# Gathering raw token rows with their moments, a norm split over VectorE and GpSimd, and a rounded output product

## The chip, the cores and the metric

The kernel runs on one core of one Trainium2 chip. The metric is the device time of the whole program in microseconds (us), taken as the median of several executions. The core has TensorE (matmuls into PSUM), VectorE, ScalarE, GpSimd and SyncE, which run their own instruction streams and meet through semaphores, and 16 DMA engines, fed here by SyncE's queue (q1) and by GpSimd's (q0). In profile rows TensorE is PE (its weight loads PEld), VectorE is DVE, ScalarE is ACT, GpSimd is POOL, SyncE is SP.

## The reference

The input x is 32 batches of 512 tokens with 256 features. With xn the layernorm of x over the features, the result is x + attention(xn) + experts(xn):

```python
xn = _layernorm(x, axis=-1)                       # (x - m) / sqrt(v + 1e-5)
# attention: 16 heads of 16, relative positions
q, k, val = heads(xn @ Wq + bq), heads(xn @ Wk + bk), heads(xn @ Wv + bv)
pos = _sinusoid_pos_emb(S, D) @ Wp + bp
score = ((q + u) @ k.T + relative_shift((q + v) @ pos.T)) / 4
att = (softmax(score) @ val) @ Wo + bo
# experts: 8, each takes its 128 best tokens of a batch
probs = softmax(xn @ gate_w); g, m = top_k(probs.T, 128)
h = gelu(xn[m] @ w1) @ w2                         # 256 -> 1024 -> 256
ffn = zeros.at[m].add(g * h)
return x + att + ffn.astype(bfloat16)
```

## The kernel before

The program has two blocks, `attention_phase` and `ffn_phase`.

**The norm stage** opens `attention_phase`: 32 steps, one batch each, over four buffers. A batch of x lies in SBUF as 128 partitions of four tokens. Per batch SyncE loads x (L335), VectorE takes statistics (L679, L682), ScalarE the root of the variance (L541), VectorE the reciprocal (L687) and then the norm, four tensor_scalars of 256 columns (L693). TensorE turns the result (8 transposes, L872), ScalarE copies it from PSUM (L548), TensorE computes expert scores (L881). SyncE stores the normed rows to `xn_d` (L339) and the turned ones to `xt_d` (L343). The normed rows in DRAM are for the expert gathers; the turned ones are read again by the attention loop. Between these steps stand, at fixed batch numbers, position projections (b 2 to 10), and the first value, query and key products (b 14 to 31). At b 6 to 9 ScalarE's copy of a spread position (L585) stands ahead of its next root in its program.

**The attention loop**, 16 iterations of two batches, goes through heads; its scores travel through DRAM for the relative shift. At its end GpSimd issues the first eight expert gathers, with VectorE, TensorE and ScalarE still at the last heads.

**The expert stage**, `ffn_phase`: 8 experts times 8 groups of four batches, so 64 groups t of 512 tokens. For a group, GpSimd gathers four times 128 rows of `xn_d` with an indirect DMA (L92), TensorE turns them (`turn`, L1535), ScalarE and VectorE split them into a rounded high part and the rest (L1390, L1432); then eight times f: the up product in three rounded partial products (L1553), gelu twice on ScalarE (L1407, L1409), a subtraction on VectorE for the low part of h (L1472), and half of a down product of the group before (L1514), whose output tile VectorE scales by the probability (L1440, every second f) and GpSimd scatters with accumulation to `ffn_d` (L1347). VectorE asks nothing of the gathers; TensorE waits for them ahead of `turn`, at f=1 of the group before.

Everything in this stage is in program order, written by hand. GpSimd's loop over t is: gather(t+2), prepare, scatter(t-1), where gather(t+2) waits for `turn` of group t and each scatter for its output tile.

Experts 1 to 4 are the mixed part: each group also carries one batch of attention output. SyncE loads heads, inverse sums and x (`load_mid`), GpSimd multiplies heads by inverse sums and adds the bias to x (`prepare`, L1353, L1354), TensorE multiplies by Wo at f=5 (`times_wo`, L1524), into the PSUM tile that `turn` uses, VectorE adds x (L1457, f=6) and SyncE stores. The product is in plain f32:

```python
ins = pe.matmul(ap[:, t], att[:, g % 2, c, t * P:(t + 1) * P], wo[:, c], start=(c == 0), stop=(c == DC - 1))
```

## Time and profile before

| | us |
|---|---|
| median of 3 runs | 4815.69 (4812.66 to 4815.7) |
| the profiled execution | 4826.3 |
| its span, first to last instruction | 4824.4 |
| TensorE busy in it | 4458.8 |
| VectorE busy | 3669.3 |
| ScalarE busy | 3441.5 |
| GpSimd busy | 1710.0 |

The norm stage runs from 0 to 147 us of the span, the attention loop's start to about 200 and the loop to 3169, the expert stage from 3175, its mixed part from about 3240 to 4100. A busy time is the union of an engine's instructions; an engine that waits inside an instruction counts as busy. Columns named "idle before" give the time in which an engine stood idle ahead of a group of instructions and what ended most of it. GB/s counts every byte that a DMA moves once.

### The profile page before, as it was taken

What the parts mean: (1) busy time and instruction counts of PE and PEld (TensorE: products, weight loads), DVE (VectorE), ACT (ScalarE), POOL (GpSimd) and SP (SyncE); (2) the same over time, 40 slices, a digit from 0 to 9 for tenths busy, and PEclk for the clock granted to TensorE, in tenths of its full rate; (3) what the DMA queues carried; (4) which work ended last, traced back from release to release, by engine and by line L of the source; (5) the groups of instructions that cost most, each with busy time, mean ns of one, the idle gap of its engine ahead of it and who ended that gap; (6) DMA issues with size and microseconds to landing.
All of it is one profiled execution on the core that took longest, in us unless ns stands there. A gap on an engine that the chain in (4) does not pass through costs nothing. (4 is left out here: it accounts for less than half of the span.)

```text
span 4824.4 us, 127659 instructions
## 1 busy us (share of the span) xinstructions
PE 4458.8 (92%) x50604; PEld 3425.4 (71%) x50604; DVE 3669.3 (76%) x8040; ACT 3441.5 (71%) x5180; POOL 1710.0 (35%) x1545
## 2 busy tenths in 40 slices
PE   7799998989999999999999989879999999999997
PEld 3466666666666666666666666669999999999997
DVE  7699999999999999999999998954554545534344
ACT  3699999999899999999898999844333434344454
POOL 0222322222232232222323222234565656544443
PEclk9899999999999999999999999989999999999999
DMA  9899999999999999999999999973555545433259
GB/s 341 334 368 377 379 374 376 376 372 378 373 383 378 378 382 375 377 377 377 372 373 379 373 372 374 365 249 65 119 135 118 146 108 145 96 63 84 48 158 316
DMA packets 394088, 1390.59 MB, mean 288 GB/s; under 512 B 51104, under 2 KB 128800, under 8 KB 327712
## 3 DMA queue, kind: packets, MB, share of 16 engines
q1 hardware_dynamic: 270624, 778.39, 44.5%
q0 software_dynamic: 122880, 604.05, 38.3%
q8 instruction: 412, 6.75, 0.6%
q14 instruction: 172, 1.41, 0.1%
HBM read 708.00 MB, written 674.23 MB: 287 GB/s over the span
## 5 line engine op out<-in xcount | busy, mean ns | idle before, releaser
L604 ACT ACTIVATE att_shifted<-att_shifted,att_mn 128x512 f32<-128x512 f32 x2048 | 1362.2, 719 | 0.2 <-DVE att_mn L740 0.2
L740 DVE CUSTOM_DVE_ANT_0 att_shifted<-att_quad,att_shifted 128x512 f32<-128x512 f32 x2048 | 1324.2, 683 | 50.1 <-PE att_quad L984 41.7
L599 ACT ACTIVATE ring<-att_quad 128x1024 f32<-128x1024 f32 x1024 | 1049.3, 1025 | 207.0 <-PE att_quad L972 204.7
L750 DVE COPY att_pt<-att_tp 128x512 f32<-128x512 f32 x1536 | 1009.8, 685 | 157.1 <-PE att_tp L1010 142.9
L490 POOL DMA_DIRECT2D att_shifted<-xs_d x512 | 279.3, 546 | 2102.5 <-DMA xs_d<-ring 1817.1
L1472 DVE TENSOR_TENSOR ffn_hp<-ring,ffn_hp 128x512 fp32r<-128x512 f32 x512 | 477.5, 933 | 686.6 <-ACT ring L1409 646.5
L1009 PEld LDWEIGHTS att_tp<-ident,att_shifted 64*128 64x128 f32 x8192 | 597.3, 140 | 517.1 <-ACT att_shifted L604 393.3
L1407 ACT ACTIVATE ffn_hp<-ffn_up 128x512 fp32r<-128x512 f32 x512 | 305.9, 597 | 915.6 <-PE ffn_up L1553 905.8
L1009 PE MATMUL att_tp<-ident,att_shifted 64*128 64x64 f32 x8192 | 727.7, 229 | 204.4 <-DVE att_pt L750 197.9
L972 PE MATMUL att_quad<-att_pos,att_qv 64*128 64x512 f32 x2048 | 870.0, 445 | 15.8 <-ACT ring L599 15.6
L984 PE MATMUL att_quad<-att_kd,att_qu 64*128 64x512 f32 x2048 | 826.7, 451 | 50.8 <-DVE att_mn L740 39.6
L1514 PE MATMUL ffn_yp<-ffn_w2p,ffn_hp 128*128 128x256 f32 x6144 | 827.8, 284 | 3.4 <-DVE ffn_hp L1472 1.7
L1514 PEld LDWEIGHTS ffn_yp<-ffn_w2p,ffn_hp 128*128 128x128 f32 x6144 | 798.7, 191 | 41.0 <-DVE ffn_hp L1472 3.8
L1553 PE MATMUL ffn_up<-ffn_xp,ffn_w1p 128*128 128x512 f32 x3072 | 795.5, 394 | 2.8 <-DVE ffn_xp L1432 2.8
L1010 PE MATMUL att_tp<-ident,att_shifted 64*128 64x64 f32 x8192 | 738.9, 231 | 2.9 <-issue 2.9
L1347 POOL DMA_INDIRECT ffn_d<-ring,picks x256 | 431.5, 1686 | 696.5 <-DVE ring L1440 683.0
L1553 PEld LDWEIGHTS ffn_up<-ffn_xp,ffn_w1p 128*128 128x128 f32 x3072 | 546.5, 190 | 93.6 <-DVE ffn_xp L1432 3.2
L1010 PEld LDWEIGHTS att_tp<-ident,att_shifted 64*128 64x128 f32 x8192 | 597.0, 140 | 4.3 <-issue 3.0
L984 PEld LDWEIGHTS att_quad<-att_kd,att_qu 64*128 64x128 f32 x2048 | 363.9, 187 | 303.2 <-DVE att_mn L740 182.2
L1027 PE MATMUL att_op<-att_pt,att_val 128*17 128x128 f32 x16384 | 564.8, 278 | 11.1 <-issue 7.1
L1027 PEld LDWEIGHTS att_op<-att_pt,att_val 128*17 128x17 f32 x16384 | 411.2, 98 | 170.6 <-issue 161.2
L972 PEld LDWEIGHTS att_quad<-att_pos,att_qv 64*128 64x128 f32 x2048 | 365.9, 186 | 68.1 <-ACT ring L599 21.6
(113 smaller groups left out, 5312.2 us busy)
## 6 DMA issues: line engine op xcount, KB each, us to landing
xs_d<-ring SPq DMA_DIRECT2D x1024, 513.0 KB, 8.9
att_shifted<-xs_d POOLq DMA_DIRECT2D x512, 1024.0 KB, 9.6
att_shifted<-in_L_attn_x_dram SPq DMA_DIRECT2D x32, 512.0 KB, 7.2
xn_d<-att_shifted SPq DMA_DIRECT2D x32, 512.0 KB, 6.3
xt_d<-att_shifted SPq DMA_DIRECT2D x32, 512.0 KB, 7.4
gathered<-xt_d SPq DMA_DIRECT2D x32, 512.0 KB, 12.1
att_d<-att_osb SPq DMA_DIRECT2D x512, 32.0 KB
ring<-in_L_ffn_w_dram SPq DMA_DIRECT2D x16, 1024.0 KB
```

Of the source, the lines that this page charges most:

```text
L599: act.activation(xo[:, kk % NW, 2 * half:2 * half + 2, 1:S + 1], xp[:, :, :], ACT.Copy).then_inc(x_out, 1)
L604: act.activation(shifted[:, kk % NX, t], shifted[:, kk % NX, t], ACT.Exp, bias=mn[:, kk % NX, t:t + 1], scale=-1.0).then_inc(exp_done, 1)
L740: dve.tensor_tensor_reduce(out=shifted[:, kk % NX, t], in0=sp_[:, t % 2], in1=shifted[:, kk % NX, t], scale=-0.25, scalar=-NEG, op0=ALU.ad ...
L750: dve.tensor_copy(turned_to(t // 2, t % 2), tp[:, t % 2]).then_inc(t_out_dve, 1)
L972: ins = pe.matmul(xp[:, t % 2, :], qv[rows, kk // GH % 2, t * P:(t + 1) * P], pos[rows, kk // GH % NG8, :], start=True, stop=True)
L984: pe.matmul(sp_[:, t % 2, :], qu[rows, kk // GH % 2, t * P:(t + 1) * P], kd[rows, kk // GH % 2, :], start=True, stop=True).then_inc(s_full, 1)
L1009: low = pe.transpose(tp[:, 0, at], shifted[0:ROWS, kk % NX, t, keys], ident[0:ROWS, 0:ROWS])
L1010: high = pe.transpose(tp[:, 1, at], shifted[ROWS:P, kk % NX, t, keys], ident[ROWS:P, ROWS:P])
L1027: ins = pe.matmul(op[32 * t:32 * t + HD + 1, kk % QH * P:(kk % QH + 1) * P], val[:, kk // H % 2, c, kk % H, :], pt[:, c, t * P:(t + 1) * P ...
L1472: dve.tensor_tensor(hp[:, g % 2, 1, f], hf[:, f % 2], hp[:, g % 2, 0, f].bitcast(F32), ALU.subtract).then_inc(h_low, 1)
L1514: ins = pe.matmul(yp[:, k % 2, 0:D], hp[:, g % 2, hi, f, k * CAP:(k + 1) * CAP], w2p[:, wi, f, :], start=(f == 0 and s == 0), stop=(f == F ...
L1553: ins = pe.matmul(up[:, f % 4, :], w1p[:, wi, c, f * P:(f + 1) * P], xp[:, g % 2, xi, c, :], start=(s == 0 and c == 0), stop=(s == 2 and c ...
```

## The change

- **Norm stage.** The normed rows are no longer stored. The mean and the inverse deviation of every token stay in a tile `st` and are stored to `st_d`, 8 bytes a token, for eight batches at a time. Of a batch's four norm instructions VectorE makes two and GpSimd two (`normed_too`). GpSimd's later work of this stage (the split of the first batch, of queries and keys) now stands between its norms, behind b=11, 24 and 27.
- **Gathers.** Each gather becomes two, of the token's moments from `st_d` and of its raw row from x.
- **Norm of gathered rows.** VectorE norms them in place, four tensor_scalars per group, for group t+2 at f=5, 6, 7 of group t; `turn` waits for them. The first two groups are normed at the end of `attention_phase`.
- **Output product.** Wo and the divided heads are split into rounded high parts (ScalarE) and low parts (VectorE), and the product is made of three partial products, 24 matmuls per batch in place of 8. The heads are split at f=0 of the group, Wo once in expert 0. `prepare` moves one group earlier.

```diff
-def gather_tokens(pool, xn_d, picks, xg, e, g, k):
-    return pool.indirect_dma_start(xg[:, g % 2, k], None, xn_d, bass.IndirectOffsetOnAxis(ap=picks[:, g * GB + k, e:e + 1], axis=0))
+def gather_tokens(pool, of_token, picks, tile, e, g, k):
+    return pool.indirect_dma_start(tile[:, g % 2, k], None, of_token, bass.IndirectOffsetOnAxis(ap=picks[:, g * GB + k, e:e + 1], axis=0))
+
+
+def normalise_tokens(dve, xg, moments, g, k):
+    of_row = moments[:, g % 2, k]
+    return dve.tensor_scalar(xg[:, g % 2, k], xg[:, g % 2, k], of_row[:, 0:1], of_row[:, 1:2], ALU.subtract, ALU.mult)
...
                 for b in range(B):
-                    store_xn(b)
                     if b + NS < B:
+                        sp.wait_ge(normed, b + 1)
+                        sp.wait_ge(normed_too, b + 1)
                         load_x(b + NS)
+                    if b % MOMENTS == MOMENTS - 1:
+                        store_moments(b + 1 - MOMENTS, b + 1)
                     if b:
                         store_xt(b - 1)
...
+                def normalise(b):
+                    k = b % NS
+                    wait_alone(pool, recip, b + 1)
+                    wait_alone(pool, turned, b - NS + 1)
+                    for t in range(TT // 2, TT):
+                        ins = pool.tensor_scalar(xn[:, k, t], xin[:, k, t], st[:, b, t, 0:1], st[:, b, t, 1:2], ALU.subtract, ALU.mult)
+                    ins.then_inc(normed_too, 1)
...
-                    dve.reciprocal(rstd[:, k], sd[:, k]).then_inc(recip, 1)
+                    dve.reciprocal(st[:, b, :, 1], sd[:, k]).then_inc(recip, 1)
                     dve.wait_ge(recip, b + 1)
 
-                    wait(dve, xn_stored[k], b // NS * 16)
                     wait(dve, turned, b - NS + 1)
-                    for t in range(TT):
-                        ins = dve.tensor_scalar(xn[:, k, t], xin[:, k, t], mv[:, k, t, 0:1], rstd[:, k, t:t + 1], ALU.subtract, ALU.mult)
+                    for t in range(TT // 2):
+                        ins = dve.tensor_scalar(xn[:, k, t], xin[:, k, t], st[:, b, t, 0:1], st[:, b, t, 1:2], ALU.subtract, ALU.mult)
                     ins.then_inc(normed, 1)
...
+                for g in range(2):
+                    dve.wait_ge(shared.x_in[g], GB * 32)
+                    for k in range(GB):
+                        normalise_tokens(dve, xg, moments, g, k).then_inc(shared.x_ready, 1)
...
                     for k in range(GB):
-                        gather_tokens(pool, xn_d, picks, xg, e, g, k).then_inc(x_in[g % 2], 16)
+                        gather_tokens(pool, st_d, picks, moments, e, g, k).then_inc(x_in[g % 2], 16)
+                        gather_tokens(pool, x.rearrange("b s d -> (b s) d"), picks, xg, e, g, k).then_inc(x_in[g % 2], 16)
...
-                    if MIX * NG <= t < MIX * NG + B:
-                        prepare(t - MIX * NG)
+                    if MIX * NG - 1 <= t < MIX * NG - 1 + B:
+                        prepare(t - (MIX * NG - 1))
...
+                def split_att(b, s):
+                    act.wait_ge(divided, b + 1)
+                    wait(act, a_full, b)
+                    act.activation(attp[:, 0], att[:, s], ACT.Copy).then_inc(a_high, 1)
...
+                def normalise(t, k):
+                    g = t % NG
+                    if k == 0:
+                        dve.wait_ge(x_in[g % 2], (t // 2 + 1) * (GB * 32))
+                    normalise_tokens(dve, xg, moments, g, k).then_inc(x_ready, 1)
...
+                def split_att(b, s):
+                    dve.wait_ge(a_high, b + 1)
+                    dve.tensor_tensor(attp[:, 1], att[:, s], attp[:, 0].bitcast(F32), ALU.subtract).then_inc(a_low, 1)
...
+                            if f >= 5 and t + 2 < NE * NG:
+                                for k in {5: (0,), 6: (1,), 7: (2, 3)}[f]:
+                                    normalise(t + 2, k)
...
-                    pe.wait_ge(divided, b + 1)
+                    pe.wait_ge(a_low, b + 1)
                     pe.wait_ge(x_low, e * NG + g + 2)
                     for t in range(TT):
-                        for c in range(DC):
-                            ins = pe.matmul(ap[:, t], att[:, g % 2, c, t * P:(t + 1) * P], wo[:, c], start=(c == 0), stop=(c == DC - 1))
+                        for n, (ai, wi) in enumerate(SPLITS):
+                            for c in range(DC):
+                                ins = pe.matmul(ap[:, t], attp[:, ai, c, t * P:(t + 1) * P], wop[:, wi, c],
+                                                start=(n == 0 and c == 0), stop=(n == 2 and c == DC - 1))
```

How the program order moves at the places that matter. First GpSimd in the norm stage, before (`att_shifted` holds x and xn, `att_xt` the split first batch, `att_qc` and `att_kc` the split queries and keys):

```order
L480 CAST att_xt<-gathered 128x1024
L482 TENSOR_TENSOR att_xt<-gathered,att_xt 128x1024
L450 CAST att_qc<-att_qn 128x512
L452 TENSOR_TENSOR att_qc<-att_qn,att_qc 128x512
L470 CAST att_kc<-att_qn 128x512
L472 TENSOR_TENSOR att_kc<-att_qn,att_kc 128x512
L450 CAST att_qc<-att_qn 128x512
L452 TENSOR_TENSOR att_qc<-att_qn,att_qc 128x512
```

and now:

```order
L514 TENSOR_SCALAR att_shifted<-att_shifted,att_st 128x256 x24
L497 CAST att_xt<-gathered 128x1024
L499 TENSOR_TENSOR att_xt<-gathered,att_xt 128x1024
L514 TENSOR_SCALAR att_shifted<-att_shifted,att_st 128x256 x26
L467 CAST att_qc<-att_qn 128x512
L469 TENSOR_TENSOR att_qc<-att_qn,att_qc 128x512
L514 TENSOR_SCALAR att_shifted<-att_shifted,att_st 128x256 x6
L487 CAST att_kc<-att_qn 128x512
L489 TENSOR_TENSOR att_kc<-att_qn,att_kc 128x512
L467 CAST att_qc<-att_qn 128x512
L469 TENSOR_TENSOR att_qc<-att_qn,att_qc 128x512
L514 TENSOR_SCALAR att_shifted<-att_shifted,att_st 128x256 x8
```

GpSimd's 64 norm instructions stand around its splits, which only followed each other before.

Second, VectorE from f=5 of a mixed group to f=1 of the next, where w2 isn't split, before (`ffn_hp` is the split h, `ring` the output tile, `ffn_tokens` x plus attention):

```order
L1472 TENSOR_TENSOR ffn_hp<-ring,ffn_hp 128x512 x2
L1440 TENSOR_SCALAR ring<-ffn_yp,chosen 128x256
L1472 TENSOR_TENSOR ffn_hp<-ring,ffn_hp 128x512
L1457 TENSOR_TENSOR ffn_tokens<-ffn_tx,ffn_tokens 128x1024
L1472 TENSOR_TENSOR ffn_hp<-ring,ffn_hp 128x512
L1440 TENSOR_SCALAR ring<-ffn_yp,chosen 128x256
```

and now (`gathered` holds the gathered rows, `ffn_attp` the split heads):

```order
L1500 TENSOR_SCALAR ring<-ffn_yp,chosen 128x256
L103 TENSOR_SCALAR gathered<-gathered,moments 128x256
L1540 TENSOR_TENSOR ffn_hp<-ring,ffn_hp 128x512
L1525 TENSOR_TENSOR ffn_tokens<-ffn_tx,ffn_tokens 128x1024
L103 TENSOR_SCALAR gathered<-gathered,moments 128x256
L1540 TENSOR_TENSOR ffn_hp<-ring,ffn_hp 128x512
L1500 TENSOR_SCALAR ring<-ffn_yp,chosen 128x256
L103 TENSOR_SCALAR gathered<-gathered,moments 128x256 x2
L1540 TENSOR_TENSOR ffn_hp<-ring,ffn_hp 128x512
L1518 TENSOR_TENSOR ffn_attp<-ffn_heads,ffn_attp 128x1024
```

Four norms and the split of the heads come in; the norm of k=1 stands ahead of the last subtraction of h.

## Rows read from the trace of the kernel before

**Rows 1.** Stretch; busy of PE, PEld, DVE, ACT, POOL; granted clock, DMA share, GB/s.

```profile
60.00:70.00 10.00, 7.50 (x18) 3.07 (x17) 4.75 (x18) 3.08 (x6) 2.32 (x1) 0.67 0.58 167
```

**Rows 2.** The same of three longer stretches.

```profile
75.00:110.00 35.00, 32.23 (x144) 15.37 (x142) 30.47 (x125) 12.91 (x21) 0.00 (x0) 1.00 1.02 413
...
3240.00:4100.00 860.00, 860.00 (x5399) 778.50 (x5398) 425.89 (x492) 332.45 (x595) 492.76 (x318) 1.00 0.52 123
4100.00:4740.00 640.00, 640.00 (x4119) 581.81 (x4118) 279.39 (x396) 282.65 (x498) 308.33 (x221) 1.00 0.43 103
```

**Rows 3.** DMA issues of the first 280 us, KB each, us to landing.

```profile
xn_d<-att_shifted SPq DMA_DIRECT2D x32, 512.0 KB, 6.3
```

**Rows 4.** Timeline of the norm stage: start, us, engine, line, idle before.

```profile
75.57 1.38 DVE L693 TENSOR_SCALAR att_shifted<-att_shifted,att_osb 128x256 f32<-128x256 f32 x4
...
78.78 1.38 DVE L693 TENSOR_SCALAR att_shifted<-att_shifted,att_osb 128x256 f32<-128x256 f32 x4
...
109.34 1.26 ACT L563 ACTIVATE att_qn<-att_mp,att_bias_q 128x512 f32<-128x512 f32 x2
...
110.76 1.25 POOL L450 CAST att_qc<-att_qn 128x512 fp32r<-128x512 f32 x1 [48.44 <-ACT att_qn L563]
...
110.98 1.18 DVE L693 TENSOR_SCALAR att_shifted<-att_shifted,att_osb 128x256 f32<-128x256 f32 x1
...
115.44 1.10 PE L872 MATMUL att_quad<-ident,att_shifted 128*128 128x128 f32 x8 [0.29 <-DVE att_shifted L693]
...
118.29 1.66 PE L911 MATMUL att_mp<-att_xt,att_wqkv 128*128 128x512 f32 x6
...
143.71 1.38 DVE L693 TENSOR_SCALAR att_shifted<-att_shifted,att_osb 128x256 f32<-128x256 f32 x4
```

**Rows 5.** Waits of the first 147 us: total, times, longest.

```profile
PE att_quad L872 <- DVE att_shifted L693: 33.7, 19, 10.1
...
DVE att_osb L679 <- DMA att_shifted<-in_L_attn_x_dram: 14.3, 14, 3.3
DVE att_osb L687 <- ACT att_osb L541: 14.0, 5, 5.3
```

**Rows 6.** Chain of waits in one mixed group: start, us, what.

```profile
3609.62 0.87 PE ffn_tx L1535 x8
...
3621.78 3.45 PE ffn_tx L1524 x16
...
3633.69 1.43 PE ffn_yp L1514 x12
...
3636.52 0.87 PE ffn_tx L1535 x8
```

**Rows 7.** Groups by line in the expert stage.

```profile
L1347 POOL DMA_INDIRECT ffn_d<-ring,picks x115 | 195.7, 1702 | 288.5 <-DVE ring L1440 282.9 <-issue 5.5
L92 POOL DMA_INDIRECT gathered<-xn_d,picks x116 | 123.5, 1065 | 35.4 <-issue 35.4
...
L1432 DVE TENSOR_TENSOR ffn_xp<-ffn_tx,ffn_xp 128x1024 fp32r<-128x1024 f32 x59 | 71.8, 1217 | 6.9 <-issue 5.1 <-ACT ffn_xp L1390 1.8
```

**Rows 8.** Timeline of the same mixed group, VectorE and GpSimd.

```profile
3614.47 5.69 DVE L1472 TENSOR_TENSOR ffn_hp<-ring,ffn_hp 128x512 fp32r<-128x512 f32 x1 [2.02 <-ACT ring L1409]
3614.84 2.42 POOL L1353 TENSOR_TENSOR ffn_heads<-ffn_heads 128x1024 f32<-128x1024 f32 x1
3617.20 2.39 POOL L1354 TENSOR_TENSOR ffn_tokens<-ffn_tokens,ffn_bob 128x1024 f32<-128x1024 f32 x1
...
3632.02 0.69 DVE L1472 TENSOR_TENSOR ffn_hp<-ring,ffn_hp 128x512 fp32r<-128x512 f32 x1 [0.99 <-ACT ring L1409]
```

**Rows 9.** GpSimd's groups in the first 280 us.

```profile
L482 POOL TENSOR_TENSOR att_xt<-gathered,att_xt 128x1024 fp32r<-128x1024 f32 x3 | 7.1, 2365 | 0.2
...
L480 POOL CAST att_xt<-gathered 128x1024 fp32r<-128x1024 f32 x3 | 3.1, 1036 | 54.9 <-DMA gathered<-xt_d 54.9
...
L470 POOL CAST att_kc<-att_qn 128x512 fp32r<-128x512 f32 x3 | 2.0, 667 | 11.6 <-ACT att_qn L570 8.9 <-PE att_mp L896 2.7
```

More of the change, by code:

```diff
@@ L154, in attention_phase @@
         xg = shared.tokens()
+        moments = shared.of_tokens()
         spread_at = (QH // GH * HD, QH // GH * HD + MH // GH * P + HD)
@@ L234, in attention_phase @@
         kept = m.sem("kept")
-        xn_stored = [m.sem(f"xn_stored{s}") for s in range(NS)]
+        st_stored = m.sem("st_stored")
+        normed_too = m.sem("normed_too")
         xt_stored = [m.sem(f"xt_stored{s}") for s in range(NS)]
@@ L490, in read_x @@
                     pool.dma_start(shifted[:, slot], xs_d[slot][S:S + S * S].rearrange("(p t c) -> p t c", t=TT, c=S)).then_inc(x_shifted[slot], 16)
-                split_xt(0, 0)
-                pool.wait_ge(p_out_dve, NG8 // 2)
-                pool.wait_ge(p_out_act, NG8 // 2)
-                with_v(0, 0)
-                keys(0, 0)
-                with_u(0, 0)
+                def normalise(b):
[5 more added lines that the diff above has]
+                    ins.then_inc(normed_too, 1)
+                for b in range(B):
+                    normalise(b)
+                    if b == 11:
+                        split_xt(0, 0)
+                    if b == 24:
+                        pool.wait_ge(p_out_dve, NG8 // 2)
+                        pool.wait_ge(p_out_act, NG8 // 2)
+                        with_v(0, 0)
+                    if b == 27:
+                        keys(0, 0)
+                        with_u(0, 0)
                 pool.wait_ge(p_low, DC)
@@ L527, in _ @@
                 pool.wait_ge(xt_low, B)
-                for n in range(NS):
-                    pool.wait_ge(xn_stored[n], 16 * (B // NS))
+                pool.wait_ge(st_stored, 16 * (B // MOMENTS))
                 by_batch = picks[:, :].rearrange("p (b e) -> p b e", e=NE)
@@ L1181, in ffn_phase @@
         att, inv = heads[:, 0:2], heads[:, 2:4]
+        sums = heads[:, 2:4].rearrange("p n c t -> p (n c t)")
         xi, mid = tokens[:, 0:2], tokens[:, 2:4]
```

66 lines of the change are left out of this document (46 added, 20 removed).

## The prediction

> **What bounds the kernel now.** I read the stages first [rows 1, 2], then in each stage the groups, the waits and the chain.
>
> The norm stage, the first 147 us, has no engine at its limit for long, but the DMA engines are: 75 to 110 us shows a DMA share of 1.02 at 413 GB/s, with TensorE at 32.2 of 35 us and VectorE at 30.5 [rows 2]. Each batch moves 512 KB three times, x in, xn out, xt out [rows 3]: 3 x 0.524 MB / 413 GB/s = 3.8 us. Eighteen batches, from VectorE's norm at 75.57 to the one at 143.71, took 68.1 us, 3.79 each [rows 4]. VectorE alone does a batch in 3.20 us (75.57 to 78.78) and waited 14.3 us in all for x [rows 4, 5]. Between 40 and 70 us another limit rules: batches 7 to 10 come slowly, because ScalarE's root of the next batch stands behind its copy of a spread position, VectorE's reciprocal waits for the root (14.0 us), and TensorE for the norm (33.7 us) [rows 5]. TensorE's granted clock is 0.67 of full as the mean of 60 to 70 us, between its levels of 1.2 and 2.4 GHz [rows 1].
>
> The attention loop (200 to 3130 us) is not touched.
>
> The expert stage belongs to TensorE: busy 860.00 of 860 us at clock 1.00 in the mixed part and 640.00 of 640 after it [rows 2]; the chain of waits there is TensorE's own matmuls, back to back [rows 6]. Whatever TensorE sheds comes off the end; whatever else is added there costs nothing unless it makes TensorE wait.
>
> **The output product, 32 times.** Before: eight f32 matmuls of 128x256, 3.45 us [rows 6]. Now 24 rounded ones with the same shape as the down product (a 128x128 weight load, 256 columns), of which twelve take 1.43 us on the chain [rows 6]: 24 x 1.43/12 = 2.86 us. Saved 0.59 us x 32 = **18.9 us**. It is on the path all of it. Bound above: the weight loads could be what paces them, but the down product has one load per matmul too, so 2.86 includes that. Bound below: nothing suggests less than 1.43/12.
>
> The product now needs more beside it. ScalarE gets a copy of 128x1024 at f=0 and VectorE a subtraction of that size, 1.22 us as the one it makes for xp [rows 7]; both have idle time there (VectorE 426 busy of 860 us, ScalarE 332 [rows 2]). The prepare on GpSimd is moved one group ahead, so that this fits: nothing.
>
> **The gathers.** Each group's four gathers become eight, four of raw rows and four of 8-byte moment rows. GpSimd needs for one gather 1.065 us and 0.31 us before it (35.4/116) [rows 7]; with the same price for the moments (same number of indices) eight take 11.0 us. Then prepare 4.8 us [rows 8], four scatters of 1.70 [rows 7] with some 0.2 between (an estimate), 7.7 us. Sum 23.5 us per mixed group, under TensorE's 26.9 - 0.6 = 26.3 us (the turn at 3609.62 to that at 3636.52 [rows 6]). The last scatter waits for the group's last output tile, so gathers start some 3 to 4 us into a group and have landed by about 17 us of it. VectorE asks for them at f=5, about 18 us in. Cover 1 to 2 us in the groups without product, more in the mixed ones: nothing on the path, but thin. Bounds: nothing, or up to 1 us a group in the 64 if landing is late and half of it shows.
>
> **The norm of gathered rows.** Four VectorE tensor_scalars per group, 1.38 us as the four in the norm stage [rows 4]. The tight place is the order at f=6: subtraction 6, the output tile, one norm, then subtraction 7, which TensorE needs for the next down product. Today it starts at 3632.02 and is done at 3632.71, TensorE comes to it at 3633.69 [rows 6, 8]: 1.0 us of slack against 0.35 us added. Where a group also splits w2 (once per expert) it can run out: I put in 0.3 us x 8, **+2 us** with the rest of such places. The first such norm, in the first group of all, waits for gathers that share the DMA with the zeroing of the accumulator in DRAM: +0 to +2, in the same figure.
>
> One behaviour matters more. In a mixed group a VectorE subtraction of two SBUF tiles that takes 0.69 us lasted 5.69 us: GpSimd's two tensor_tensors ran from 3614.84 to 3619.59, and it ended 0.57 us after them [rows 8]. So VectorE stood still for whole GpSimd instructions. It is hidden now (TensorE did not pause), and moves from f=3 to about f=5, where the product's 2.86 us cover it.
>
> **The norm stage.** Removed: 32 stores of 512 KB, so DMA needs 2 x 0.524/413 = 2.54 us per batch; SP loses 32 issues and gains four small ones. The limit passes to an engine. TensorE needs 2.85 us per batch: the turn starts at 115.44, the scores follow, and the next product starts at 118.29 [rows 4]. VectorE gives two of four tensor_scalars (0.69 us) to GpSimd. If both could run at once it would need 2.5 us. But they read SBUF at once: with GpSimd's cast in front of it (110.76 to 112.01) one VectorE tensor_scalar lasted 1.18 us instead of 0.35 [rows 4]. Both shares start from the same reciprocal, VectorE right behind it, GpSimd some 0.16 us later (the time from ScalarE's end, 110.60, to GpSimd's cast, 110.76 [rows 4]), so VectorE's second one waits for both of GpSimd's: 0.16 + 2P + 0.1 + 0.34 = 2P + 0.6 us, in place of 1.38, and a batch is 3.20 - 1.38 + 0.6 + 2P = 2.42 + 2P.
>
> P, a GpSimd tensor_scalar of 256 columns, stands in no row. Nearest are its casts, 667 ns for 512 columns and 1036 for 1024 [rows 9]: 0.72 ns a column and 0.30 fixed, so 0.48 us. Lower bound: VectorE's own 0.35. Upper: as two-input ops go, 2.37 us for 1024 columns [rows 9], some 0.7 for 256. I take 0.48, as it has one tensor input like the cast. Then 3.38 us per batch, 18 x 3.38 = 60.8. GpSimd's splits for queries and keys (2.8 and 4.7 us, now between two norms) hold VectorE's share up for some 5.5 us more than now: 66.3 against 68.1, -1.8. Before batch 13: the fifth load of x is issued 0.4 us earlier and lands without stores beside it, -2; the four serial batches keep their 1.38 us of norm as 1.56, +0.7. With the last stores gone in front of the first positions -1. **Sum -4 us**; with P at 0.35 it is -9, with 0.7 it is +4.
>
> The GPSIMD Engine Reference of the Trainium skill (section "When to use GPSIMD") calls one-input elementwise work on GpSimd roughly line-rate with VectorE; by it P would be near 0.35 and the sum 5 us lower, while the cast rows speak for 0.48.
>
> **The hand-over to the experts.** Sixteen gathers in place of eight, 22 us instead of 11, lie beside attention's last heads, and VectorE's eight norms, 2.8 us, beside its last stores. Nothing, bounds -2 and +3.
>
> **Sum.** -18.9 + 2 - 4 = -21 us. The profiled execution took 4826.3 us (span 4824.4), so 4805; the median of the runs is 10.6 us under it, and I predict from that: 4815.7 - 21 = **4794.5 us**, -0.44%.
>
> **Rivals.**
> A. Norm stage at TensorE's pace (17%). For it: TensorE was busy 92% at 75 to 110 us. Against: the 1.18 us row. 18 x 2.85 + 5 for its extra products (6 of them, the one at 118.29 takes 1.5) = 56 against 68, with the start -13: total -30, 4786.
> B. GpSimd's share is slow and the norm stage longer (15%). For it: VectorE stands still for all of it. P = 0.7 to 1.0 gives 3.8 to 4.4 us per batch, +4 to +15 us: total -13 to -2, 4803 to 4814.
> C. GpSimd's queue becomes the bound of the mixed part, slower than before (5%). Place: gathers, prepare and scatters in one queue, 23.5 of 26.3 us. It decides from (26.3 - 12.5)/8 = 1.72 us per gather with its gap, against 1.37 in the rows. If gathers cost what scatters do (1.70 + 0.3), a group is 28.5 us, 1.6 more than now: +51 - 4, 4863. Against: it needs 45% more per gather. The page "DMA: Bandwidth & Descriptors" of the Trainium skill (quick facts) wants 512 bytes or more per transfer, below which it speaks of a read-modify-write. No row here shows what an 8-byte row costs; it would burden the landing, and so the thin cover above.
> D. The product doesn't shrink (3%): three times the weight loads eat what the rounding saves. It stays at 3.45 us, total +2 - 4, 4814; against it the down product's 1.43.
> The forecast itself has 60%.
>
> **How the numbers follow.** A measurement tells about 0.2% (9.6 us) from no change. The forecast's own range: -9 to +4 in the norm stage for -4, 0 to 6 for the 2, so 4788 to 4803. The range that leaves out no more than C, D and the ends of A and B: 4781 to 4811. Faster by over 0.2% (under 4806): all of the forecast, A, a third of B: 0.81. Within: the rest of B and D, 0.13. Slower: C and what I don't see, 0.06.
>
> **What would show it.** Right: 24 matmuls of the product in about 2.86 us; TensorE busy all of the mixed part, groups 26.3 us apart; norms of the first stage 3.4 us apart after batch 12, with no wait of the statistics for x and VectorE tensor_scalars stretched to 1 us or more; DMA share there near 0.75. Wrong: TensorE idle before its turn or down product (late gathers), GpSimd without idle time in the mixed part, norms 4 us apart or 2.9, or a product of 3.4 us.

## The result, and the profile after

| | before | changed |
|---|---|---|
| median, us | 4814.17 (4 runs, 4807.62 to 4815.7) | 5234.77 (4 runs, 5232.59 to 5239.27) |
| span of the profiled execution, us | 4824.4 | 5234.9 |
| mean granted clock of TensorE | 0.982 | 0.933 |

The ratio is **1.0879**, 95% interval 1.0867 to 1.0892: 8.8% slower, where 0.44% faster was forecast. The time lies outside the range of 4781 to 4811.

I cut each execution at two instructions of TensorE: its first score product and its first transposition in the experts. These two rows are from the timeline of the changed kernel (start us, us, engine, line; idle before):

```profile
190.33 0.79 PE L1017 MATMUL att_quad<-att_kd,att_qu 64*128 64x512 f32 x1
...
3589.78 1.94 PE L1612 MATMUL ffn_tx<-ident,gathered 128*128 128x128 f32 x8 [6.41 <-PEq L343]
```

And of the kernel before:

```profile
182.25 0.71 PE L984 MATMUL att_quad<-att_kd,att_qu 64*128 64x512 f32 x1
...
3175.66 1.94 PE L1535 MATMUL ffn_tx<-ident,gathered 128*128 128x128 f32 x8 [6.57 <-PEq L330]
```

Up to the scores: 182.3 before, 190.3 now, +8.0. The loop between the two rows: 2993.4 before, 3399.5 now, **+406**. The experts, from there to the end of the span: 1648.7 before, 1645.1 now, -3.6. So nearly all of the loss is in the loop, which the change edits nowhere and of which the prediction says one sentence.

The stretches of the changed kernel, beside [rows 2] (busy of PE, PEld, DVE, ACT, POOL; granted clock, DMA share, GB/s):

```profile
75.00:110.00 35.00, 31.41 (x134) 15.00 (x135) 31.34 (x113) 11.17 (x20) 28.20 (x22) 0.90 0.83 262
400.00:3000.00 2600.00, 2226.32 (x30727) 1561.97 (x30727) 2153.42 (x5130) 2087.12 (x3004) 655.15 (x738) 0.92 1.02 330
3660.00:4500.00 840.00, 837.93 (x5569) 768.05 (x5570) 490.45 (x650) 357.51 (x623) 613.37 (x442) 1.00 0.51 124
```

The stretch of the loop in the kernel before:

```profile
400.00:3000.00 2600.00, 2366.78 (x35006) 1661.31 (x35006) 2427.30 (x5817) 2372.71 (x3422) 748.19 (x843) 0.99 1.02 376
```

The DMA share is 1.02 in both: the loop keeps all the DMA engines occupied, before and now. But before they moved 376 GB/s in that time, and now 330. Every engine did less in the same 2600 us (35006 matmuls against 30727). The page of the changed kernel shows what got slower, in its groups and its DMA issues (the last number is us to landing):

```profile
L507 POOL DMA_DIRECT2D att_shifted<-xs_d x512 | 279.3, 545 | 2505.9 <-DMA xs_d<-ring 2290.8
...
xs_d<-ring SPq DMA_DIRECT2D x1024, 513.0 KB, 10.8
att_shifted<-xs_d POOLq DMA_DIRECT2D x512, 1024.0 KB, 10.9
...
gathered<-xt_d SPq DMA_DIRECT2D x32, 512.0 KB, 15.7
```

The page of the kernel before:

```profile
L490 POOL DMA_DIRECT2D att_shifted<-xs_d x512 | 279.3, 546 | 2102.5 <-DMA xs_d<-ring 1817.1
...
xs_d<-ring SPq DMA_DIRECT2D x1024, 513.0 KB, 8.9
att_shifted<-xs_d POOLq DMA_DIRECT2D x512, 1024.0 KB, 9.6
...
gathered<-xt_d SPq DMA_DIRECT2D x32, 512.0 KB, 12.1
```

The loop writes each head's position scores to the scratch array xs_d in device memory and reads them back shifted by one place per row. The same transfers of the same sizes land 1.3 to 3.6 us later. Between 500 and 2900 us the packets of 8192 B have a median of 309 ns in both traces; what grew is the share of packets that take over twice the median, from 5.0% to 11.5%. The instructions of VectorE, ScalarE and GpSimd took as long as before, within 1% in the mean of that stretch; TensorE's matmuls took 72 ns instead of 68, at a granted clock of 0.92 instead of 0.99. What got slower in the first place is a memory access. The edit had done one thing to the loop's arrays: the first of the DRAM arrays, xn_d with 16 MiB, became st_d with 128 KB, so all later ones start elsewhere. Besides, the shared tile moments pushed ring and the tiles behind it 64 B further in SBUF.

### The profile page after: what moved, and what is told of

It is laid out like the page before. It is cut to its first block and busy times, and to the rows that moved or that the text cites. A ratio compares the mean times of both kernels' runs of the same rounds, so it can differ in the third digit from the quotient of the medians.

```text
span 5234.9 us, 128805 instructions
## 1 busy us (share of the span) xinstructions
PE 4626.4 (88%) x50860; PEld 3544.6 (68%) x50860; DVE 3783.0 (72%) x8265; ACT 3474.4 (66%) x5213; POOL 2043.4 (39%) x1865
## 5 line engine op out<-in xcount | busy, mean ns | idle before, releaser
L1017 PE MATMUL att_quad<-att_kd,att_qu 64*128 64x512 f32 x2048 | 891.4, 475 | 226.2 <-DVE att_mn L768 216.5
L1042 PEld LDWEIGHTS att_tp<-ident,att_shifted 64*128 64x128 f32 x8192 | 643.6, 148 | 487.2 <-ACT att_shifted L633 320.7
L1042 PE MATMUL att_tp<-ident,att_shifted 64*128 64x64 f32 x8192 | 781.5, 238 | 185.6 <-DVE att_pt L778 172.7
L1005 PE MATMUL att_quad<-att_pos,att_qv 64*128 64x512 f32 x2048 | 912.6, 467 | 24.5 <-ACT ring L628 24.0
L1540 DVE TENSOR_TENSOR ffn_hp<-ring,ffn_hp 128x512 fp32r<-128x512 f32 x512 | 431.9, 847 | 552.5 <-ACT ring L1459 418.5
L1630 PE MATMUL ffn_up<-ffn_xp,ffn_w1p 128*128 128x512 f32 x3072 | 796.9, 395 | 10.2 <-ACT ring L1459 7.4
L1043 PE MATMUL att_tp<-ident,att_shifted 64*128 64x64 f32 x8192 | 784.3, 240 | 1.8 <-issue 1.6
L1017 PEld LDWEIGHTS att_quad<-att_kd,att_qu 64*128 64x128 f32 x2048 | 392.3, 199 | 462.5 <-DVE att_mn L768 343.1
L1043 PEld LDWEIGHTS att_tp<-ident,att_shifted 64*128 64x128 f32 x8192 | 641.1, 148 | 15.0 <-issue 9.5
L1060 PE MATMUL att_op<-att_pt,att_val 128*17 128x128 f32 x16384 | 624.6, 298 | 27.9 <-issue 17.1
L1060 PEld LDWEIGHTS att_op<-att_pt,att_val 128*17 128x17 f32 x16384 | 439.6, 104 | 223.7 <-issue 190.2
L1005 PEld LDWEIGHTS att_quad<-att_pos,att_qv 64*128 64x128 f32 x2048 | 387.4, 198 | 106.8 <-issue 36.9
```

The costliest lines, as they stand in the source:

```text
L1005: ins = pe.matmul(xp[:, t % 2, :], qv[rows, kk // GH % 2, t * P:(t + 1) * P], pos[rows, kk // GH % NG8, :], start=True, stop=True)
L1017: pe.matmul(sp_[:, t % 2, :], qu[rows, kk // GH % 2, t * P:(t + 1) * P], kd[rows, kk // GH % 2, :], start=True, stop=True).then_inc(s_full, 1)
L1042: low = pe.transpose(tp[:, 0, at], shifted[0:ROWS, kk % NX, t, keys], ident[0:ROWS, 0:ROWS])
L1043: high = pe.transpose(tp[:, 1, at], shifted[ROWS:P, kk % NX, t, keys], ident[ROWS:P, ROWS:P])
L1060: ins = pe.matmul(op[32 * t:32 * t + HD + 1, kk % QH * P:(kk % QH + 1) * P], val[:, kk // H % 2, c, kk % H, :], pt[:, c, t * P:(t + 1) * P ...
L1540: dve.tensor_tensor(hp[:, g % 2, 1, f], hf[:, f % 2], hp[:, g % 2, 0, f].bitcast(F32), ALU.subtract).then_inc(h_low, 1)
```

## The experiments: why the loop is slower

Three theories: **M**, the place in device memory; **S**, the place in SBUF; **O**, the order or the waits of the change.

**a_dram**, the changed kernel:

```diff
-    st_d = nc.dram_tensor("st_d", [B * S, 2], F32).ap()
+    st_d = nc.dram_tensor("st_d", [B * S * D], F32).ap()[:B * S * 2].rearrange("(n m) -> n m", m=2)
```

> The changed kernel with st_d declared at the size that xn_d had (16.8 MB, of which its 128 KB are used), so that every later DRAM array lies where it lay in the kernel before; nothing else differs. Theory M (the attention loop became slower because xt_d, xs_d and att_d lie elsewhere in device memory, so the same packets take longer): the loop goes back to 376 GB/s and ends some 410 us earlier, 4820 us +-20 in all. Theory S (the new tiles in SBUF moved ring and the attention tiles): no change, 5235 us. Theory O (order or waits of the change itself slow the loop): no change, 5235 us.

Measured 4804.44 us beside 4807.0 of the kernel before. Its loop:

```profile
400.00:3000.00 2600.00, 2370.03 (x35010) 1662.05 (x35008) 2426.77 (x5817) 2371.49 (x3421) 746.35 (x842) 0.99 1.02 376
```

The loss is gone with one declaration, and the loop took 2983.2 us. M holds, O falls.

**a_sbuf**, the changed kernel, and **b_sbuf**, the kernel before:

```diff
-        self.moments = sb("moments", 2 * GB * 2)
         self.ring = sb("ring", 4 * TT * (S + 1))
+        self.moments = sb("moments", 2 * GB * 2)
```

```diff
+        self.pad = sb("pad", 2 * GB * 2)
         self.ring = sb("ring", 4 * TT * (S + 1))
```

> The changed kernel with the shared tile moments (64 B per partition) declared behind ring, so that ring starts where it did in the kernel before. Theory S: the loop goes back to 376 GB/s, 4820 us +-20 if ring's start is what counts; the tiles of the attention phase still stand 64 B further. Theory M and theory O: 5235 us, the loop at 331 GB/s.

> The kernel before with an unused tile of 64 B per partition ahead of ring, so that ring and every later tile start 64 B further, as in the changed kernel. Theory S: the loop falls to some 331 GB/s and the time rises to 5220 us +-30. Theories M and O: 4814 us +-15.

Measured 5387.15 and 4825.81 us beside 4807.0; loops at 315 and 376 GB/s. S falls twice. That a_sbuf is another 150 us slower than the changed kernel was in no expectation. The tile's place is not needed for it: a_st_xs below has the tiles of the changed kernel and comes out at 5416.11. Why the changed kernel moved 330 GB/s in the loop and three others with the same start of xs_d 314 or 315 is open; its own four executions lie within 7 us.

**b_dram**: in the kernel before, the declaration of xn_d moved behind that of mid_d.

> The kernel before with xn_d declared behind the other DRAM arrays instead of ahead of them: xt_d, ffn_d, xs_d, att_d and the rest then start 16.8 MB earlier, nearly where they start in the changed kernel (there 128 KB of st_d lie ahead). Theory M: the loop slows, up to 5225 us (less if only the 128 KB offset counts). Theories S and O: 4814 us +-15.

Measured 4822.75 us, 377 GB/s. A move by 16 MiB leaves the rate alone; of what the changed kernel moved, the 128 KB remain.

The next four shift arrays by 128 KB. **a_st_last**, **a_st_xs** and **a_st_att**: in the changed kernel, the line that declares st_d moved behind mid_d, ahead of xs_d, or ahead of att_d. **b_128k**, the kernel before:

```diff
-    xn_d = nc.dram_tensor("xn_d", [B * S, D], F32).ap()
+    xn_d = nc.dram_tensor("xn_d", [B * S * D + B * S * 2], F32).ap()[:B * S * D].rearrange("(n d) -> n d", d=D)
```

> The changed kernel with st_d (128 KB) declared last of the DRAM arrays, so that xt_d is the first and everything starts 128 KB lower than in the changed kernel, 16 MiB lower than in the kernel before. Theory O (the 128 KB offset of the other arrays is what slows the loop; a shift by 16 MiB cost at most 16 us): 4805 us +-15, loop at 376 GB/s. Theory R (it is the missing 16 MiB ahead of them that counts in the changed kernel): 5235 us +-30.

> The kernel before with 128 KB more declared behind xn_d (unused), so that xt_d, ffn_d, xs_d, att_d and the rest start 128 KB higher, and nothing else. Theory O: slow, 5215 us +-40, with no other part of the change in it. Theory R: 4814 us +-15.

> The changed kernel with st_d declared between ffn_d and xs_d: xt_d and ffn_d start on multiples of 16 MiB from the first, xs_d, att_d and the rest 128 KB higher. Theory XS (the placing of xs_d, through which the loop writes and reads its rows, is what counts): 5235 us +-40. Theory XT (where xt_d lies counts, since it is read by the loop beside xs_d): 4805 us +-15.

> The changed kernel with st_d declared between xs_d and att_d: only att_d, sums_d, inv_d and mid_d start 128 KB higher. Theory XS and theory XT: 4805 us +-15. If att_d, to which the loop writes its sums of values, is what counts: 5235 us +-40.

Measured, beside 4824.29 for the kernel before: a_st_last 4851.65 (375 GB/s), a_st_att 4848.42 (375), a_st_xs **5416.11** (314), b_128k **5390.39** (315). The last is the plainest: the kernel before, with no part of the change but 128 KB of unused memory, and the loss is there in full.

```profile
400.00:3000.00 2600.00, 2157.57 (x29270) 1507.46 (x29267) 2058.10 (x4896) 1992.45 (x2865) 623.09 (x703) 0.89 1.02 315
```

The expectations were right in which kernels are slow, and too narrow in size: the two slow ones took some 180 us more than 5215 to 5235, the two others 24 to 27 us more than the kernel before beside them. Moving att_d and what follows by 128 KB leaves the rate at 375 GB/s. The only array that a_st_xs moves and a_st_att leaves is xs_d: its start decides.

**a_xs_pad**, the changed kernel, tests this from the other side: the rows of xs_d are put back, and with them att_d and the arrays behind it; xt_d and ffn_d stay where the change put them.

```diff
-    xs_d = nc.dram_tensor("xs_d", [S * P + 8 * S * (S + 1)], F32).ap()[S * P:].rearrange("(k n) -> k n", k=8)
+    xs_d = nc.dram_tensor("xs_d", [S * P // 2 + 8 * S * (S + 1)], F32).ap()[S * P // 2:].rearrange("(k n) -> k n", k=8)
```

> The changed kernel with the unused stretch that xs_d keeps ahead of its rows cut from 256 KB to 128 KB. With the 128 KB of st_d ahead, the rows of xs_d and att_d then start where they do in the kernel before (less 16 MiB), while xt_d and ffn_d stay 128 KB off. Theory XS (only where the rows of xs_d start counts): 4805 us -15/+45, loop at 370 GB/s or more. Rival (a second array, xt_d or ffn_d, off its place is as bad): above 5200 us.

Measured 4814.89 us, ratio 0.9981 (0.9970 to 0.9992), 376 GB/s. xt_d and ffn_d, still 128 KB off, don't matter, and with a_st_att neither does a shift of att_d by 128 KB.

Which starts are slow? **b_pad512**, **b_pad0**, **b_pad128** and **b_pad640** are the kernel before with that unused stretch at 512, 0, 128 and 640 KB instead of 256.

> The kernel before with the unused stretch ahead of the rows of xs_d widened from 256 KB to 512 KB; att_d and what follows move up by 256 KB too. If starts at odd multiples of 128 KB are the bad ones: 4814 us +-40. If the slow down grows with the distance from 256 KB: above 5380 us (128 KB more gave 5390). If nothing but this start is fast: some 5200 to 5400 us.

> The kernel before with no unused stretch ahead of the rows of xs_d (0 instead of 256 KB). Known so far, as the distance of these rows from the grid of 16 MiB: 256 KB and 512 KB fast, 384 KB slow. Odd theory (odd multiples of 128 KB are slow, even ones fast): 4820 us +-25. Band theory (a band around 384 KB is slow, the rest fast): 4820 us too. Chance theory (each start has its own collisions): anything from 4800 to 5400 us.

> The kernel before with 128 KB ahead of the rows of xs_d. Odd theory: slow, 5200 to 5420 us. Band theory: 4820 us +-25. Chance theory: anything.

> The kernel before with 640 KB ahead of the rows of xs_d. Odd theory: slow, 5200 to 5420 us. Band theory: 4820 us +-25. Chance theory: anything.

| rows of xs_d start at, past a multiple of 16 MiB | kernels | GB/s from 400 to 3000 us | us |
|---|---|---|---|
| 0 | b_pad0 | 316 | 5380 |
| 128 KB | b_pad128 | 316 | 5375 |
| 256 KB | before, a_dram, b_sbuf, b_dram, a_st_last, a_st_att, a_xs_pad | 375 to 377 | 4804 to 4852 |
| 384 KB | changed, a_sbuf, b_128k, a_st_xs | 314 to 330 | 5235 to 5416 |
| 512 KB | b_pad512 | 376 | 4817 |
| 640 KB | b_pad640 | 337 | 5171 |

The odd theory and the band theory both fall with b_pad0. Both said 4820 us for it, and it took 5380. Four of six starts are slow, and I have no rule for which, nor for how slow: at one and the same start, 384 KB, both 330 and 314 GB/s were measured. The starts 0, 128, 512 and 640 KB rest on a single execution of the kernel before each (bp_pad512, below, has 512 KB too, at 375 GB/s), and these four also move att_d and the arrays behind it, by other distances than the 128 KB of a_st_att. The start is counted here as the declarations lay the arrays out one behind the other; the profile shows no addresses.

The page "DMA: Bandwidth & Descriptors" of the Trainium skill (section "Latency and other measured facts") reports transfers that lose up to half their rate when the pitch of their rows in device memory is a large power of two, and gives colliding channels as an unverified inference. The runs here agree that a layout in device memory sets the rate, but go further than that rule: pitches and sizes are the same in all of them, and the start alone makes 376 or 315 GB/s. No run here varied a pitch, so the cause behind the start stays open.

## The experiments: what the change is worth in its place

**a_dram5** is a_dram again, timed.

> The kernel of a_dram again, timed: the whole change with its arrays where they lay before, GpSimd sharing the norm. Its one look was 4804 beside a before of 4807; by stages it was 6.0 us later at the first score product, 17.6 us shorter in the experts. Theory P: some 6 to 12 us above g_norm_dve (0.9958), so 0.997 to 0.999 of before. Rival (the norm stage's end is made up for later): 0.9958 +-0.001.

Measured **1.0037** (1.0023 to 1.0051), 4847.92 us beside 4829.46, above both theories. But a_xs_pad, the same change with the loop repaired in another way and run on another chip, took 0.9981 (0.9970 to 0.9992) of the kernel before there. So with the loop repaired the change is worth between -0.2% and +0.4%, and not the -0.44% of the forecast. Whether the chip or the other placement makes the sign is not shown; 8 us of the difference are the stops in the first expert groups, of which below. Three kernels take it apart.

**g_norm_dve**: a_dram, with all four norms of a batch on VectorE and GpSimd's loop of norms and its semaphore gone.

```diff
-                    for t in range(TT // 2):
+                    for t in range(TT):
                         ins = dve.tensor_scalar(xn[:, k, t], xin[:, k, t], st[:, b, t, 0:1], st[:, b, t, 1:2], ALU.subtract, ALU.mult)
```

> The changed kernel with st_d declared at the size of xn_d (the placement of the kernel before), and all four norms of a batch on VectorE, none on GpSimd. VectorE then has 4x0.35 + 0.38 + 0.15 + 4x0.45 = 3.7 us of work per batch, under the 3.8 us that a batch took before. Theory P (the norm stage of the changed kernel lost its gain to GpSimd's 1.3 us per quarter): the last transposition of x ends near 146 us or earlier instead of 152.6, TensorE's waits for GpSimd in the stage are gone, and the time is 0 to 6 us below the 4804 of the shared norm. Rival (the stage is bound by something else, or what follows waits for other work until 195 us anyway): no change, 4804 us +-3.

Measured 0.9958 (0.9942 to 0.9974), 4802.53 us, on the chip on which a_xs_pad took 4814.89; theory P holds, with the last transposition of x done at 141.8 us, and at 157.6 in a_xs_pad. The two shares of a batch look like this in the changed kernel (timeline):

```profile
88.91 0.90 DVE L721 TENSOR_SCALAR att_shifted<-att_shifted,att_st 128x256 f32<-128x256 f32 x2
88.98 2.56 POOL L514 TENSOR_SCALAR att_shifted<-att_shifted,att_st 128x256 f32<-128x256 f32 x2 [0.29 <-DVE att_st L716]
...
90.73 1.41 DVE L708 BATCH_NORM_STATS2 att_osb<-att_shifted 128x6 f32<-128x256 f32 x4 [0.92 <-DMA att_shifted<-in_L_attn_x_dram]
...
92.65 0.90 DVE L721 TENSOR_SCALAR att_shifted<-att_shifted,att_st 128x256 f32<-128x256 f32 x2
```

Its groups by line, first 160 us:

```profile
L514 POOL TENSOR_SCALAR att_shifted<-att_shifted,att_st 128x256 f32<-128x256 f32 x64 | 82.4, 1295 | 56.3 <-DVE att_st L716 56.2
```

The same stage in g_norm_dve, its stretch and its timeline:

```profile
75.00:110.00 35.00, 34.37 (x153) 16.31 (x151) 34.29 (x134) 13.81 (x24) 2.35 (x2) 1.00 0.99 315
```

```profile
98.37 1.38 DVE L706 TENSOR_SCALAR att_shifted<-att_shifted,att_st 128x256 f32<-128x256 f32 x4
...
101.58 1.38 DVE L706 TENSOR_SCALAR att_shifted<-att_shifted,att_st 128x256 f32<-128x256 f32 x4
```

One norm on GpSimd takes 1.295 us, on VectorE 0.35. The next load of x into a buffer waits for both shares, so it starts later, and VectorE's statistics wait about 1 us for x. With VectorE alone the two batches shown are 3.21 us apart (98.37 to 101.58). From the norm of batch 13 to that of batch 31 g_norm_dve took 62.2 us and a_xs_pad, on the same chip, 66.8. But most of the loss lies earlier: batch 13's norm starts at 74.7 us in the one and at 85.9 in the other. The reason is given under the norm stage in the section on why the prediction was wrong. The first score product starts at 176.8 us instead of 192.7.

**b_product**: the kernel before with the output product of the change (attp, wop, their splits, 24 matmuls, prepare one group ahead), and nothing else of it.

> The kernel before with only the output product in rounded parts: normed rows written and gathered as before, no moments, no norm in the experts. Left as it is in both: everything up to the experts. My sum has 18.9 us for the product and 2 us of cost for the norm of gathered rows; the changed kernel with its arrays in place took 838.7 us for the 32 mixed groups against 854.7. Theory A (product 18.9, norm of gathered rows costs 3): here 836 us for the 32 groups, 4795 us. Theory B (the product itself gives 16, the norm is free): 838.7 us for the 32 groups, 4798 us, no other difference to before.

Measured **0.9951** (0.9937 to 0.9965), 4798.19 us. The 32 mixed groups took 837.5 us, from the first to the last start of ScalarE's split of xp in them, against 854.7 before. That is between the two theories: the product gives 17.2, and beside the 838.7 us of a_dram the norm of gathered rows costs 1.2. Its chain of waits (start, us, what), beside [rows 6]:

```profile
3625.83 2.87 PE ffn_tx L1556 x24
3628.70 1.44 PE ffn_yp L1545 x12
```

**g_raw**: g_norm_dve with the product as before and `prepare` back in its own group, so raw rows and moments alone.

> Raw rows alone: as g_norm_dve (placement of the kernel before, all norms of the first stage on VectorE, moments and raw rows gathered and normed in the experts), but with the output product in float32 as in the kernel before. From the rows so far: the first stage ends 5.4 us earlier than before, the experts take about 3 to 6 us more (g_norm_dve 1635 us, b_product 1629). Theory Z (raw rows are worth nothing in sum, the gain is the product's): 0.998 to 1.001 of before. Rival (raw rows gain and the product's gain is smaller beside them): 0.995 to 0.997.

Measured **1.0059** (1.0044 to 1.0074), 4856.44 us: both theories missed. The raw rows cost, instead of being worth nothing. By stages (span 4859.6, not on the same chip as the trace of before): scores start at 181.75, -0.5; the loop takes 3007.4, +14.0; the experts 1670.4, +21.7. The experts' part, by the starts of ScalarE's split of xp: the first eight groups 158.4 us against 146.8, the mixed ones 859.9 against 854.7 (the second of each mixed expert takes 27.9 instead of 26.9), the later ones 572.0 against 569.6, and what follows 2.4 more. The slow mixed group is not the change's: in it TensorE waits 0.26 us for a subtraction and 0.75 for GpSimd's division of the heads, once in each of the four experts, while in the changed kernel, where `prepare` comes a group earlier, only the 0.26 are there. The first groups in g_raw (timeline of TensorE):

```profile
3199.20 7.10 PE L1581 MATMUL ffn_up<-ffn_xp,ffn_w1p 128*128 128x512 f32 x30
3209.75 1.74 PE L1581 MATMUL ffn_up<-ffn_xp,ffn_w1p 128*128 128x512 f32 x6 [3.46 <-issue]
3215.45 2.90 PE L1581 MATMUL ffn_up<-ffn_xp,ffn_w1p 128*128 128x512 f32 x6 [3.95 <-ACT ring L1428]
```

And of ScalarE, in the same stretch:

```profile
3208.53 0.60 ACT L1426 ACTIVATE ffn_hp<-ffn_up 128x512 fp32r<-128x512 f32 x1 [4.38 <-remote]
...
3214.22 0.60 ACT L1426 ACTIVATE ffn_hp<-ffn_up 128x512 fp32r<-128x512 f32 x1 [4.61 <-remote]
```

In b_product TensorE ran 42 of these matmuls without a stop:

```profile
3169.76 9.78 PE L1586 MATMUL ffn_up<-ffn_xp,ffn_w1p 128*128 128x512 f32 x42
```

ScalarE stood for something that the profile doesn't name, while the DMA engines were full with the zeroing of ffn_d and the gathers (413 GB/s from 3195 to 3224 us; but g_norm_dve, without a stop, moved 408 at the same place). TensorE's two stops shown here and two later ones (2.09 and 2.36 us) add up to 11.9 us, about the 11.6 that the first groups lost. The first eight groups took 157 to 158 us in the changed kernel and in all kernels with raw rows on two of the chips (a_st_last, a_st_xs, a_st_att; a_dram5, g_raw), and 147 to 149 in all of them on two others (a_dram, a_sbuf; a_xs_pad, g_norm_dve). No kernel without raw rows had the stop (145 to 147 us, b_128k beside the first three among them). So g_norm_dve and g_raw, timed on different chips, can't be subtracted from each other. What ScalarE waited for is open. A late fetch of instructions is not borne out: the trace has a queue q8 whose packets it calls instruction, and none of them ran in g_raw from 3195 to 3224 us, which holds all but the last of these stops.

**bp_pad512**: b_product with 512 KB ahead of the rows of xs_d.

> The kernel before with the output product in rounded parts and 512 KB instead of 256 KB ahead of the rows of xs_d. The product alone gave 0.9951 of before. If the 512 KB start is a little better than the 256 KB one (one look: 4817 beside a before of 4824, the loop 8 us shorter), 0.993 to 0.995; if that was scatter, 0.9951 +-0.0015. Slower than before only if the 512 KB start were bad in other runs.

Measured 0.9966 (0.9951 to 0.9980): the 512 KB start brings nothing more. b_product has the lowest time of all, 0.9951. g_norm_dve and bp_pad512 beat the kernel before too, and their intervals overlap with its own, so which of the three is best is not shown.

| profiled execution | first scores at | loop | experts | span |
|---|---|---|---|---|
| before | 182.3 | 2993.4 | 1648.7 | 4824.4 |
| changed | 190.3 | 3399.5 | 1645.1 | 5234.9 |
| a_dram | 188.3 | 2983.2 | 1631.2 | 4802.6 |
| a_dram5 | 192.3 | 2996.8 | 1645.3 | 4834.4 |
| g_norm_dve | 176.8 | 2987.1 | 1635.1 | 4799.1 |
| b_product | 180.1 | 2979.9 | 1629.3 | 4789.3 |
| g_raw | 181.8 | 3007.4 | 1670.4 | 4859.6 |

Loops at 375 to 377 GB/s differ by up to 28 us in this table, and by 36 with all traces (2979.9 in b_product, 3015.4 in a_st_last), without a cause that I could find, and the first scores of kernels with the norm stage of before lie between 178.6 and 188.7 us. Four of these ran on one chip and lie between 181.4 and 188.7 there, so a comparison on one chip does not remove the scatter. Single traces tell nothing under some 10 us in the first stage and 30 in the loop.

## Why the prediction was wrong, step by step

**"The attention loop (200 to 3130 us) is not touched": the step that failed.** It was true of the instructions and false of the time. The profile showed that the loop is bound by memory traffic (a DMA share of 1.02 at 376 GB/s), and the diff showed that the first of eight DRAM arrays shrank by 16 MiB less 128 KB. I put the two nowhere together, and gave the loop neither a term nor a rival. What the runs showed in its place: the start of xs_d sets the rate of the loop, 330 GB/s instead of 376, and 128 KB of unused memory in the kernel before are enough for it (b_128k, 5390.39 us). It cost +406 us; no other term reached 20. Why this start is slow stays open.

**The output product, -18.9 us: right.** It takes 2.87 us on the chain where 2.86 was forecast, mixed groups are 26.3 us apart, and b_product saved 17.2 us in them (the 1.7 missing were not traced). Alone it gives 0.9951.

**The norm stage, -4 us: wrong in sign.** Forecast P was 0.48 us with 0.7 as its upper bound; it is 1.295. The bound was taken from casts and two-input operations of 512 and 1024 columns [rows 9], none with a scalar per partition, so the interval didn't hold. The other half of the model failed too: VectorE did not stand still for GpSimd's norms, its two took 0.90 us beside GpSimd's 2.56, against 1.38 for four before.

Where batches overlap, the two errors worked against each other. From the norm of batch 13 to that of batch 31 the changed kernel took 65.1 us (85.8 to 150.9, 3.6 a batch) and the kernel before 68.1: -3.0, for -1.8 forecast. By the formula with the measured P, 2.42 + 2P, it would have been 5.0 us a batch. That this part came out near the forecast is luck.

The loss is before batch 13, which starts 10.2 us later (85.8 against 75.6), and nearly all of it in the four serial batches, 7 to 10. From the norm of batch 6 to that of batch 10 they took 39.6 us (34.9 to 74.5), before 30.5 (34.9 to 65.4). I had put +0.7 there. Every one of them goes from the root of the variance through the norm, the transpositions and the positions to the next root, so the slower share stands on the path in full. TensorE's transpositions in the changed kernel (timeline; idle before):

```profile
46.42 1.94 PE L905 MATMUL att_quad<-ident,att_shifted 128*128 128x128 f32 x8 [3.79 <-issue]
```

and in the kernel before:

```profile
42.84 1.97 PE L872 MATMUL att_quad<-ident,att_shifted 128*128 128x128 f32 x8 [2.50 <-DVE att_shifted L693]
...
50.97 1.09 PE L872 MATMUL att_quad<-ident,att_shifted 128*128 128x128 f32 x8 [2.50 <-DVE att_shifted L693]
```

The wait is 1.29 us longer, 5.2 in four batches. The rest goes with TensorE's granted clock: the same eight transpositions take 1.94 us where it is 0.50 (46.4 to 48.3 us of the changed kernel; its lower level, 1.2 GHz) and 1.09 where it is 1.00 (51.0 to 52.1 us of the kernel before; 2.4 GHz). The stretch from 35 to 75 us in the changed kernel, the kernel before, b_dram and b_128k, in this order (clock, DMA share and GB/s at the end):

```profile
35.00:75.00 40.00, 25.50 (x71) 10.56 (x69) 14.93 (x50) 7.68 (x13) 11.68 (x9) 0.74 0.45 145
35.00:75.00 40.00, 29.10 (x97) 13.46 (x96) 25.82 (x91) 9.38 (x17) 3.37 (x2) 0.83 0.80 274
35.00:75.00 40.00, 26.50 (x76) 12.07 (x75) 23.91 (x76) 8.17 (x15) 3.37 (x2) 0.73 0.67 234
35.00:75.00 40.00, 29.36 (x110) 13.28 (x111) 29.99 (x111) 11.32 (x20) 3.39 (x2) 0.91 0.89 314
```

b_dram and b_128k have the norm stage of before and did the four serial batches in 35.1 and 26.2 us; the ten kernels with that stage lie along this line, from 0.91 to 0.72. At 0.72 to 0.74 four of them took 35.1 to 35.4 us, and five with the shared norm 39.0 to 40.3: that is what the sharing costs at the same clock, some 4 to 5 us. Whether the longer waits also bring the low clock about, which all eight kernels with the shared norm had (0.73 to 0.81), is open. Over all traces the first scores start at 188.3 to 192.7 us in these eight (mean 190.5) and at 178.6 to 188.7 in the ten (mean 183.9).

Rival B had a slow GpSimd, with too small a P, and priced it by a VectorE that stands still for all of it. Its +4 to +15 us hold the measured +8 by another way, through the serial batches. The GPSIMD Engine Reference of the Trainium skill (section "When to use GPSIMD") and its rough line rate are further off than my 0.48: the trace disagrees by a factor of 3.7 (1.295 against 0.35).

What the stage could have given is what g_norm_dve shows: 176.8 us, 3.3 us before b_product on the same chip, and 15.8 before a_xs_pad; between batches 13 and 31 it took 62.2 us and b_product 67.7. The removed stores are the gain, and the sharing took it away with interest.

**The gathers and norms in the experts, +2 us: the places were right, one was missing.** Eight gathers take 8 x (1.03 + 0.30) = 10.6 us for 11.0 forecast, and GpSimd was not the bound (rows of the changed kernel, 3660 to 4500 us):

```profile
L98 POOL DMA_INDIRECT moments<-st_d,picks x128 | 131.8, 1029 | 39.0 <-issue 39.0
L98 POOL DMA_INDIRECT gathered<-in_L_attn_x_dram,picks x128 | 130.4, 1019 | 39.0 <-issue 39.0
```

An issue for 8-byte rows costs what one for 1 KB rows does. The tight place at f=6 is there, at its forecast price: in the group that splits w2, TensorE waits 0.26 us for a subtraction that stands behind a norm, in each of the four mixed experts, not in all eight (timeline of the changed kernel, where 0.3 was put in):

```profile
4027.49 1.69 PE L1589 MATMUL ffn_yp<-ffn_w2p,ffn_hp 128*128 128x256 f32 x12 [0.26 <-DVE ffn_hp L1540]
```

What was sized "+0 to +2" is the first groups: they cost 10 to 12 us in six of ten traces, and 0 to 3 in the other four. So with product and raw rows together the experts take 1631 to 1635 us where the stops are missing and 1644 to 1646 where they are, against 1629.3 in b_product: raw rows cost them 2 to 17 us, at worst about all that the product gains. The four mixed waits, 1.0 us, are most of the 1.2 us that the mixed groups lose.

**The hand-over, 0: right.** TensorE's first transposition there follows a stop of 6.41 us, 6.57 before.

**The chances.** All four rivals were about the terms I had named. None of them went above 4863 us, since none had the loop in it. "What I don't see" shared 6% with rival C, which had 5 of them: 1% was left for it, in a kernel whose largest stage runs at the limit of a shared resource. The forecast's own range had a slip besides: -18.9 + 4 + 6 ends at 4807, not at 4803.

## What to carry to other kernels

Where a stage keeps the DMA engines full with traffic through a scratch array in device memory, the start of that array is a parameter of the kernel like a tile size: whoever adds, removes or resizes a DRAM array declared ahead of it has to look at that stage's GB/s again, before the change itself is judged. Put new arrays last, or at the size of the one they replace. And a part of a norm is worth giving to GpSimd only with the duration of that very operation at hand, and with the question who waits for the slower of the two shares: where batches follow each other without overlap, all of it is paid.

## What the runs showed of the hardware that was not expected

- The start of xs_d changes the rate of the loop: 375 to 377 GB/s at 256 and 512 KB, 337 at 640, 314 to 330 at 0, 128 and 384 KB, at a DMA share of 1.01 to 1.02 throughout. The share of busy time does not tell good from bad; GB/s does. The median of the packets does not tell it either.
- A GpSimd tensor_scalar of 128x256 float32 with two scalars per partition takes 1.295 us, longer than its cast of 128x1024 (1.036 us, [rows 9]), and slows VectorE's beside it by about a third (0.90 us for two, against 1.38 for four), while a GpSimd tensor_tensor of 128x1024 held a VectorE subtraction for its whole length [rows 8].
- TensorE's granted clock in the slow loop is 0.89 to 0.93, with more waits in it, and 0.99 in the fast one; so TensorE spends part of the slow loop at the lower of its levels, 1.2 instead of 2.4 GHz. No run separates what this costs; the rate follows the start of xs_d in every run.
